# Layer normalisation on ScalarE's accumulator instead of VectorE's statistics, in a kernel with hand-written engine orders

## The chip, the cores and the metric
The kernel runs on one core of a Trainium2 chip. The metric is the device time of one execution in microseconds; three executions of the kernel before took 2475.67 to 2481.44 us, median 2475.96 us.

## The reference
A batch of 32 sequences with 256 tokens of 128 features passes through four blocks, each added to its input and each reading a layer-normalised copy of it:

```python
def _layernorm(x, axis=-1, eps=1e-05):
    m = jnp.mean(x, axis=axis, keepdims=True)
    v = jnp.var(x, axis=axis, keepdims=True)
    return (x - m) / jnp.sqrt(v + eps)

x = x + attention_0(_layernorm(x))   # 8 heads of one token mixed with each other, complex-valued encoding
x = x + ffn_0(_layernorm(x))         # silu(gate) * up, hidden size 384
x = x + attention_1(_layernorm(x))   # causal attention, 16 heads of 8, 256 tokens
x = x + ffn_1(_layernorm(x))         # 8 experts, each takes its 64 best tokens of a sequence
```

## The kernel before, in words
A sequence is held as two tiles of 128 tokens (partitions) by 128 features; T = 2 is the number of tiles. There are three parts: a setup of weights, a loop over the 32 sequences (here called batches), and an expert stage for the last block, which begins when all sequences have been through the loop.

The loop is a software pipeline of five stages: A (normalisation, projection to q, k, v, encoding and three layers of gates), C (the rest of the first attention, up to x1), B (first FFN, up to x2, and the normalisation of x2), E (scores, exponents and values of the second attention) and D (its output, x3, the normalisation of x3 and the routing logits). In one pass of the loop A works on batch b, C on b-1, B on b-2, E and D on b-3. Each stage is written as one Python generator for each engine; a `yield` ends a piece. Four strings set the order in which the pieces of the stages stand in the queue of an engine: `DVE_ORDER`, `ACT_ORDER`, `POOL_ORDER`, `PE_ORDER` ("C1A1C1" is one piece of C, one of A, one of C). Each engine runs its queue in that order, and waits on semaphores for the others. `together` unrolls the strings, `sequences` makes the loop with four passes ahead of it and three behind it. The numbers `DVE_A_STEPS` and so on count the increments of a semaphore that a stage uses on VectorE against itself.

A normalisation, before: VectorE runs `bn_stats` on each tile of the source, a small memset that keeps distance, and `bn_aggr` on each (mean and variance); GpSimd (`norm_scale`, L456) adds eps, negates the mean, raises to the power -0.5 and multiplies; ScalarE (`norm_apply`, L465) applies scale and bias. There are four a batch: A of the input (`x_land`), B1 of x1, B2 of x2, and D of x3.

Names used below: w0 to w7 are the eight products of the weighted sums (`weighted`, L627), six of them on VectorE and numbers 3 and 7 on GpSimd; TensorE sums each over the heads (L751), in the PSUM tile `pa`. L637 and L638 clip the result for each tile, L759 is the output projection, L612 writes x1. diag, add, ctrl and stadd are L522, L525, L527 and L529 of gate layers 1 and 2 on VectorE; cross and ctrl on GpSimd are L657 and L662, and they deliver what add and ctrl on VectorE need. state0 is L505, which waits for the power L649 on GpSimd. In E, `exp` is L923 and L924, a turn is L1036 on TensorE with the copy L931 on ScalarE, a maximum is L810 and L811 on VectorE. In D, L830 writes x3, L1086 transposes its normalised tile `xn_d`, L958 copies that, L1091 makes the logits. `pa` is shared by A, C and B, and semaphores take it from one to the next.

Of the kernel before, what the change touches and what calls it, by code (L numbers as in the profile page):

```python
# [27 lines left out]
EPS = 1e-5  # L28
SIGN = 0x80000000
# [19 lines left out]
POOL_ORDER = "A1C2B1A4C1B1A2C1D1C1D1"  # L49
ACT_ORDER = "E7A1E1A1E3A1E5B1E4B1E3C1A1E2B1E3C1E3B1A1E2C1E6A1E1B1D1C1D1C1D2"  # L50
PE_ORDER = "E4A1E1A1E6B1E4B1E7B1E2B1E3C1E1C1E1C1E1C1D1C1D1C1D1C2D2C2"
DVE_ORDER = "C1A1C1A1C1B1C1E1B1E1C2A1E1C1A1C1E1C2E1C2A1C1E1A1C1B1C1B1A1C1E1A1C2B1C1B1C1E1B1A1C1A1C2B2A2C2A1D2C2D3C1A2C2D2A1D2A1C1"


def build(nc, A, out):
# [8 lines left out]
    with ctx:  # L64
        def sb(name, shape, dt=F32):
            return ctx.enter_context(nc.sbuf_tensor(name, shape, dt))
# [80 lines left out]
        stats_a = first("stats_a", [P, T, 6])  # L147
        mv_a = first("mv_a", [P, T, 2])
# [33 lines left out]
        stats_b = first("stats_b", [P, T, 6])  # L182
        mv_b = first("mv_b", [P, T, 2])
# [9 lines left out]
        stats_d = first("stats_d", [P, T, 6])  # L193
        mv_d = first("mv_d", [P, T, 2])
# [280 lines left out]
        def vector_a(v, b):  # L475
            count_a[0] = 0
            L = lambda ins: link_a(v, b, ins)

            v.wait_ge(S("x_in"), 16 * b + 16)
            for t in range(T):  # L480
                count_a[0] += 1
                v.bn_stats(stats_a[:, t, :], x_land[:, t, :]).then_inc(S("dve_a"), 1)
            yield
            v.wait_ge(S("dve_a"), b * DVE_A_STEPS + 2)

            v.memset(spare[:, 3:4], 0.0).then_inc(S("dve_a"), 1)
            count_a[0] += 1
            for t in range(T):
                count_a[0] += 1
                v.bn_aggr(mv_a[:, t, :], stats_a[:, t, :]).then_inc(S("dve_a"), 1)  # L490
            yield
# [273 lines left out]
        def vector_norm(v, b, n, src):  # L765
            k0 = count_b[0]
            for t in range(T):
                count_b[0] += 1
                v.bn_stats(stats_b[:, t, :], src[:, t, :]).then_inc(S("dve_b"), 1)
            yield  # L770
            v.wait_ge(S("dve_b"), b * DVE_B_STEPS + k0 + 2)

            v.memset(spare[:, n:n + 1], 0.0).then_inc(S("dve_b"), 1)
            count_b[0] += 1
            for t in range(T):
                count_b[0] += 1
                v.bn_aggr(mv_b[:, t, :], stats_b[:, t, :]).then_inc(S("dve_b"), 1)
# [36 lines left out]
        def vector_d(v, b):  # L814
# [18 lines left out]
            v.wait_ge(S("x3_ready"), b + 1)  # L833
            for t in range(T):
                count_d[0] += 1
                v.bn_stats(stats_d[:, t, :], x3[:, t, :]).then_inc(S("dve_d"), 1)
            yield
            v.wait_ge(S("dve_d"), b * DVE_D_STEPS + 3)

            v.memset(spare[:, 2:3], 0.0).then_inc(S("dve_d"), 1)  # L840
            count_d[0] += 1
            for t in range(T):
                count_d[0] += 1
                v.bn_aggr(mv_d[:, t, :], stats_d[:, t, :]).then_inc(S("dve_d"), 1)
            yield

# [15 lines left out]
        def gpsimd_b(g, b):  # L862
            for n in range(2):
                g.wait_ge(S("dve_b"), b * DVE_B_STEPS + (5, 12)[n])
                norm_scale(g, 2 * b + n, mv_b, var_b, rstd_b, shift_b, "b_scale", "b_rstd")
                yield

        def gpsimd_d(g, b):
            g.wait_ge(S("dve_d"), b * DVE_D_STEPS + 6)
            norm_scale(g, b, mv_d, var_d, rstd_d, shift_d, "d_scale", "d_rstd")  # L870
# [573 lines left out]
```

## Time and profile before

| | |
|---|---|
| median of 3 runs | 2475.96 us |
| the profiled execution | 2466.69 us |
| its span, first to last instruction | 2464.9 us |
| busy TensorE / VectorE / ScalarE / GpSimd | 79% / 77% / 52% / 55% |
| mean granted TensorE clock | 0.902 |
| in the loop (1000 to 1500 us): VectorE, TensorE | 453.5 and 417.7 us of 500 |

The busy time is the sum of the durations of an engine's instructions; consecutive ones can overlap, so an engine may be free a little more than the difference suggests. The loop lasts until about 2080 us; the expert stage follows. Idle time in front of an instruction is put down to the instruction of another engine that released it last.

### The profile page before, as it was taken

How to read it: one execution, taken by the hardware profiler on the slowest of the kernel's cores; microseconds unless marked ns; L12 is line 12 of the kernel's file. 1: busy time of each engine (PE TensorE's matmuls, PEld its weight loads, DVE VectorE, ACT ScalarE, POOL GpSimd, SP SyncE). 2: the span in 40 equal slices, each digit the busy share in tenths (PEclk: the TensorE clock that was granted, in tenths of full speed). 3: DMA queues.
4: the chain of work that ended last, by engine and by line, in shares of the span. 5: the costliest groups of instructions: out<-in, count | busy, mean ns of one | idle time of the engine just before them, and what ended most of it. 6: DMA issues, size and time to landing. Idle time of an engine off the chain costs nothing.

```text
span 2464.9 us, 45044 instructions
## 1 busy us (share of the span) xinstructions
PE 1951.1 (79%) x15068; PEld 1517.4 (62%) x15068; DVE 1904.4 (77%) x3422; ACT 1272.1 (52%) x2989; POOL 1357.8 (55%) x1104
## 2 busy tenths in 40 slices
PE   1357888888888888888888888888888886199999
PEld 0346666666666666666666666666666663167777
DVE  4899999998999999899889999999988843402221
ACT  1126666655566655556555556665555554043332
POOL 2666666666666666666666666666666310544400
PEclk9679999988999988999988999998898896599999
DMA  3000000000000000000000000000000000112210
GB/s 93 3 7 9 10 11 9 9 9 9 9 9 9 9 9 9 9 9 9 9 9 9 9 9 9 9 9 9 9 9 6 7 6 9 45 33 69 61 42 26
DMA packets 64565, 39.38 MB, mean 16 GB/s; under 512 B 9350, under 2 KB 60431, under 8 KB 64528
## 3 DMA queue, kind: packets, MB, share of 16 engines
q1 hardware_dynamic: 54238, 26.30, 3.7%
q0 software_dynamic: 4096, 8.40, 1.3%
q10 hardware_dynamic: 6194, 4.21, 0.7%
q8 instruction: 21, 0.34, 0.1%
q14 instruction: 16, 0.13, 0.0%
HBM read 26.31 MB, written 12.58 MB: 16 GB/s over the span
## 4 chain that ended last, share of the span: by engine, by line
PE 27%; issue 22%; POOL 21%; DVE 20%; ACT 6%; ACTq 1%; DVEq 1%; POOLq 0%; DMA 0%
POOL arena L461 5%; PE pa L1296 5%; PE pd L1286 5%; POOL arena L657 5%; POOL arena L629 4%; DVE arena L811 4%; PE pb L1036 3%; POOL arena L458 2%; PE pa L732 2%; POOL arena L662 2%; POOL arena L463 1%; PE pa L759 1%; DVE arena L563 1%; POOL arena L1223 1%; DVE arena L558 1%
## 5 line engine op out<-in xcount | busy, mean ns | idle before, releaser
L751 PE MATMUL pa<-ident,arena 128*128 128x128 f32 x4096 | 528.9, 286 | 54.8 <-DVE arena L629 53.2
L751 PEld LDWEIGHTS pa<-ident,arena 128*128 128x128 f32 x4096 | 500.7, 200 | 72.6 <-DVE arena L629 36.5
L1036 PE MATMUL pb<-ident,arena 128*128 128x128 f32 x1536 | 292.7, 304 | 122.2 <-ACT arena L931 111.9
L1036 PEld LDWEIGHTS pb<-ident,arena 128*128 128x128 f32 x1536 | 188.4, 154 | 243.8 <-issue 158.5
L931 ACT ACTIVATE arena<-pb 128x384 f32<-128x384 f32 x512 | 252.3, 493 | 161.2 <-PE pb L1036 156.8
L657 POOL TENSOR_TENSOR arena<-state,c_cross 128x448 f32<-128x448 f32 x128 | 204.9, 1620 | 209.0 <-DVE state L518 204.7
L649 POOL TENSOR_TENSOR arena<-arena,neg_half 128x32 f32<-128x32 f32 x64 | 264.9, 4158 | 83.8 <-DVE arena L495 83.8
L629 POOL TENSOR_TENSOR arena<-arena 128x1024 f32<-128x1024 f32 x64 | 149.0, 2329 | 194.3 <-PE pa L751 194.3
L924 ACT ACTIVATE arena<-pd,arena 128x256 f32<-128x256 f32 x512 | 244.9, 478 | 0.0
L629 DVE TENSOR_TENSOR arena<-arena 128x1024 f32<-128x1024 f32 x192 | 236.5, 1257 | 2.9 <-PE pa L751 2.7
L458 POOL TENSOR_TENSOR arena<-arena,eps_t 128x2 f32<-128x2 f32 x128 | 106.0, 828 | 221.3 <-DVE arena L490 135.3
L923 ACT ACTIVATE arena<-pd,arena 128x128 f32<-128x128 f32 x512 | 188.5, 368 | 59.6 <-DVE arena L811 56.5
L1223 POOL DMA_INDIRECT arena<-xn_scratch,arena x128 | 122.0, 953 | 139.8 <-PE pa L1276 76.1
L1235 DVE TENSOR_TENSOR arena<-pa,arena 128x512 f32<-128x512 f32 x32 | 22.1, 692 | 221.5 <-PE pa L1296 221.5
L461 POOL TENSOR_TENSOR arena<-arena,neg_half 128x2 f32<-128x2 f32 x128 | 170.0, 1328 | 10.0
L811 DVE TENSOR_REDUCE arena<-pd 128x2 f32<-128x512 f32 x256 | 174.1, 680 | 0.0
L1027 PE MATMUL pd<-arena 32*128 32x256 f32 x1024 | 161.2, 392 | 0.0
L810 DVE TENSOR_REDUCE arena<-pd 128x2 f32<-128x256 f32 x256 | 106.3, 415 | 56.7 <-PE pd L1027 56.5
L559 DVE TENSOR_REDUCE arena<-arena 128x128 f32<-128x2048 f32 x64 | 146.0, 2281 | 0.1
L1266 ACT ACTIVATE arena<-pd,b 128x512 f32<-128x512 f32 x128 | 87.9, 687 | 108.9 <-PE pd L1286 108.4
L669 POOL TENSOR_TENSOR arena<-arena,state 128x1024 f32<-128x1024 f32 x64 | 131.4, 2075 | 0.7 <-DVE arena L553 0.7
L1024 PE MATMUL pd<-arena 32*128 32x128 f32 x1024 | 131.7, 335 | 0.0
(246 smaller groups left out, 4374.6 us busy)
## 6 DMA issues: line engine op xcount, KB each, us to landing
x_land<-in_L_attn_query SPq DMA_DIRECT2D x32, 128.0 KB, 2.1
arena<-in_L_attn_query SPq DMA_DIRECT2D x32, 128.0 KB, 2.1
x_scratch<-x SPq DMA_DIRECT2D x32, 128.0 KB, 1.8
xn_scratch<-xn_d SPq DMA_DIRECT2D x32, 128.0 KB, 1.8
arena<-x_scratch SPq DMA_DIRECT2D x16, 256.0 KB, 3.0
out_x<-arena SPq DMA_DIRECT2D x16, 256.0 KB, 2.4
w<-in_L_ffn_W ACTq DMA_DIRECT2D x1, 2048.0 KB
arena<-xn_scratch,arena POOLq DMA_INDIRECT x128, 2.5
```

The source lines that it names most:

```text
L458: g.tensor_tensor(var[:, :], mv[:, :, 1], eps_t[:, :], ALU.add).then_inc(S(steps), 1)
L461: g.tensor_tensor(rstd[:, :], var[:, :], neg_half[:, 0:2], ALU.pow).then_inc(S(steps), 1)
L629: return eng.tensor_tensor(wprod[:, k % NWP, :].rearrange("p (j i d) -> p j i d", j=NH, d=HD), amps[:, c, t, :, :].rearrange("p i j -> p j ...
L649: g.tensor_tensor(of_tile(rnorm)[:, :, c], of_tile(ssq)[:, :, c], of_tile(neg_half)[:, :, c], ALU.pow).then_inc(S("a_rnorm"), 1)
L657: ins = g.tensor_tensor(gate_r[:, c, :, :], st[:, 1 - c, :, HD:E], c_cross[:, l, 0:GW].unsqueeze(1).broadcast_to([P, 4, GW]), ALU.mult)
L751: mm = pe.matmul(pa[:, t, c * P:c * P + P], wprod[:, k % NWP, j * 128:j * 128 + 128], ident[:, :], start=(j == 0), stop=(j == NH - 1))
L811: v.tensor_reduce(n_max[:, 1, 2 * n:2 * n + 2], pd[:, s, 128:384], AX, ALU.min).then_inc(S("b_m"), 1)
L923: act.activation(p[:, 0:128], bank[:, 0:128], ACT.Exp, bias=n_max[:, 0, s:s + 1], scale=-1.0)
L924: act.activation(p[:, 128:384], bank[:, 128:384], ACT.Exp, bias=n_max[:, 1, s:s + 1], scale=-1.0)\
L931: act.activation(p_t[:, s % 8, :], pb[:, 0:384], ACT.Copy).then_inc(S("b_pt"), 1)
L1027: mm = pe.matmul(o[:, 128:384], q_m[rows_of, r, P:2 * P], k_t[rows_of, :], start=False, stop=True, skip_group_check=True)
L1036: mm = pe.transpose(pb[:, j * P:j * P + P], p_raw[:, s % 3, j * P:j * P + P], ident[:, :])
```

## The change
`bn_stats`, `bn_aggr` and the memset leave VectorE. ScalarE gets two passes over each tile instead: a Copy with the accumulator gives the sum, then a Square of x/sqrt(128) - mean/sqrt(128) with the accumulator gives the variance. Their elementwise outputs go to the tile that the normalised values overwrite later. GpSimd makes the mean between the two passes (`norm_mean`), and `norm_scale` loses the negation. Where a normalisation was one piece on GpSimd and one on ScalarE, it is now two and three. All four order strings are new.

```diff
-DVE_A_STEPS = 15
+DVE_A_STEPS = 10
 DVE_C_STEPS = 19
-DVE_B_STEPS = 12
-DVE_D_STEPS = 8
-POOL_ORDER = "A1C2B1A4C1B1A2C1D1C1D1"
-ACT_ORDER = "E7A1E1A1E3A1E5B1E4B1E3C1A1E2B1E3C1E3B1A1E2C1E6A1E1B1D1C1D1C1D2"
-PE_ORDER = "E4A1E1A1E6B1E4B1E7B1E2B1E3C1E1C1E1C1E1C1D1C1D1C1D1C2D2C2"
-DVE_ORDER = "C1A1C1A1C1B1C1E1B1E1C2A1E1C1A1C1E1C2E1C2A1C1E1A1C1B1C1B1A1C1E1A1C2B1C1B1C1E1B1A1C1A1C2B2A2C2A1D2C2D3C1A2C2D2A1D2A1C1"
+DVE_B_STEPS = 2
+DVE_D_STEPS = 3
+POOL_ORDER = "A1B1A1C1B1C1A4C1B1A1B1C1D1A1D1C1D1"
+ACT_ORDER = "E2B1A1E4A1E1B1E3A1E3A1B1E2A1E1B1E4C1E3A1E1B1E2C1E4A1B1E3C1E3B1E4B1C1A1D1B1D3C1D2"
+PE_ORDER = "E6A1E2A1E2B1E5B1E7B1E2B1E3C1E1C1E1C1E1C1D1C1D2C3D2C2"
+DVE_ORDER = "C4E1C1E1C2E1C1A2E1C4E1C2A1C1A1E1B1C1A1B1A1C2E1C1B2C1A1E1B1C3A1C1A1C1A1D2C1D1C2A3C2D2A1D1A1C1D1"
...
-        def norm_scale(g, u, mv, var, rstd, shift, steps, done):
-            g.tensor_tensor(var[:, :], mv[:, :, 1], eps_t[:, :], ALU.add).then_inc(S(steps), 1)
-            g.tensor_tensor(shift[:, :], mv[:, :, 0], minus_one[:, :], ALU.mult).then_inc(S(steps), 1)
+        def norm_sums(act, src, dst, total, done):
+            for t in range(T):
+                act.activation(dst[:, t, :], src[:, t, :], ACT.Copy, accum_out=total[:, t:t + 1]).then_inc(S(done), 1)
+        def norm_mean(g, total, shift, mean, steps, done):
+            g.tensor_tensor(shift[:, :], total[:, :], by_mean[:, :], ALU.mult).then_inc(S(steps), 1)
+            g.tensor_tensor(mean[:, :], total[:, :], by_scaled_mean[:, :], ALU.mult).then_inc(S(done), 1)
+        def norm_squares(act, src, dst, mean, var, done):
+            for t in range(T):
+                act.activation(dst[:, t, :], src[:, t, :], ACT.Square, bias=mean[:, t:t + 1], scale=ROOT_E,
+                               accum_out=var[:, t:t + 1]).then_inc(S(done), 1)
+        def norm_scale(g, u, var, rstd, shift, steps, done):
+            g.tensor_tensor(var[:, :], var[:, :], eps_t[:, :], ALU.add).then_inc(S(steps), 1)
             g.wait_ge(S(steps), 3 * u + 2)
             g.tensor_tensor(rstd[:, :], var[:, :], neg_half[:, 0:2], ALU.pow).then_inc(S(steps), 1)
             g.wait_ge(S(steps), 3 * u + 3)
             g.tensor_tensor(shift[:, :], shift[:, :], rstd[:, :], ALU.mult).then_inc(S(done), 1)
...
         def gpsimd_a(g, b):
-            g.wait_ge(S("dve_a"), b * DVE_A_STEPS + 5)
-            norm_scale(g, b, mv_a, var_a, rstd_a, shift_a, "a_scale", "a_rstd")
+            g.wait_ge(S("a_sums"), 2 * b + 2)
+            norm_mean(g, total_a, shift_a, mean_a, "a_scale", "a_mean")
+            yield
+            g.wait_ge(S("a_squares"), 2 * b + 2)
+            norm_scale(g, b, var_a, rstd_a, shift_a, "a_scale", "a_rstd")
             yield
...
         def scalar_a(act, b):
+            act.wait_ge(S("x_in"), 16 * b + 16)
+            norm_sums(act, x_land, xn_a, total_a, "a_sums")
+            yield
+            act.wait_ge(S("a_mean"), b + 1)
+            norm_squares(act, x_land, xn_a, mean_a, var_a, "a_squares")
+            yield
             act.wait_ge(S("a_rstd"), b + 1)
             norm_apply(act, x_land, rstd_a, shift_a, xn_a, "a_xn")
```

B1, B2 and D are changed in the same way. With the new strings the pieces stand as follows around the end of a pass. VectorE, new: w0 w1 w2 add1 w4 ctrl1 w5 stadd1, reciprocal, o_n, w6, x3, clip of tile 0 (two pieces), diag2 add2 ctrl2, clip of tile 1, logits maximum, stadd2, r_sum, v_enc, x1, r_inv. VectorE, before: w0 add1 w1 w2, statistics B2, ctrl1 stadd1 w4 w5 diag2, reciprocal, o_n, w6, L637, x3, statistics D, L638, add2 ctrl2, clip of tile 1, and on as above, with x1 last. GpSimd, new: mean A, mean B1, scale A, third product 0, scale B1, third product 1, two powers, cross1, ctrl1, w3, mean B2, cross2, scale B2, w7, mean D, ctrl2, scale D. GpSimd, before: scale A, two third products, scale B1, two powers, cross1, ctrl1, w3, scale B2, cross2, ctrl2, w7, scale D. ScalarE, new, at the start of a pass: copy of x2, copy of the transposed tile, sums B1, sums A, four copies of k and q, squares A, v, squares B1, exp0, exp1, turn 0, apply A; at its end: last turn, o_raw, squares B2, L719, gate square 2, o_t, apply B2, sums D, squares D, apply D.

## Rows read from the trace of the kernel before

**Rows 1.** The page's engine totals for the whole span.
```profile
PE 1951.1 (79%) x15068; PEld 1517.4 (62%) x15068; DVE 1904.4 (77%) x3422; ACT 1272.1 (52%) x2989; POOL 1357.8 (55%) x1104
```
**Rows 2.** The line that writes x1; busy time of one period (windows).
```profile
L612 DVE TENSOR_TENSOR arena<-arena,pa x32: 414/422/423, 125.6 to 1993.0; 128x256 f32<-128x256 f32 x32
...
1086.80:1147.40 60.60, 49.40 (x395) 38.52 (x396) 55.97 (x98) 36.05 (x89) 39.18 (x30) 0.95 0.03 9
```
**Rows 3.** Waits, 1026 to 1511 us: total, times, longest.
```profile
PE pd L1086 <- ACT xn_d L467: 11.5, 8, 1.6
...
DVE arena L612 <- PE pa L759: 9.3, 7, 1.6
```
**Rows 4.** Timeline of VectorE, 1058 to 1120 us: start, duration, instruction.
```profile
1060.02 1.21 DVE L629 TENSOR_TENSOR arena<-arena 128x1024 f32<-128x1024 f32 x1
...
1065.10 2.23 DVE L527 TENSOR_TENSOR arena<-arena 128x896 f32<-128x896 f32 x1
1067.37 1.10 DVE L529 TENSOR_TENSOR state<-state,arena 128x896 f32<-128x896 f32 x1
...
1076.37 0.42 DVE L830 TENSOR_TENSOR x<-arena,pd 128x256 f32<-128x256 f32 x1 [0.33 <-PE pd L1081]
1076.82 0.49 DVE L836 BATCH_NORM_STATS2 arena<-x 128x6 f32<-128x128 f32 x2
...
1077.51 0.66 DVE L638 SCALAR_TENSOR_TENSOR arena<-pa,arena 128x512 uint32<-128x512 uint32 x1
...
1086.34 0.42 DVE L612 TENSOR_TENSOR arena<-arena,pa 128x256 f32<-128x256 f32 x1 [1.35 <-PE pa L759]
...
1087.50 0.48 DVE L482 BATCH_NORM_STATS2 arena<-x_land 128x6 f32<-128x128 f32 x2
1087.90 0.41 DVE L555 TENSOR_TENSOR arena<-state 128x256 f32<-128x256 f32 x1
...
1097.76 0.95 DVE L494 TENSOR_REDUCE arena<-arena 128x48 f32<-128x768 f32 x1 [0.76 <-ACT arena L693]
...
1108.17 0.69 DVE L505 TENSOR_TENSOR state<-arena 128x512 f32<-128x512 f32 x1
```
**Rows 5.** Timeline of GpSimd, same stretch.
```profile
1066.34 1.04 POOL L458 TENSOR_TENSOR arena<-arena,eps_t 128x2 f32<-128x2 f32 x1
...
1069.62 4.05 POOL L657 TENSOR_TENSOR arena<-state,c_cross 128x448 f32<-128x448 f32 x2
1073.64 2.12 POOL L662 TENSOR_TENSOR arena<-arena 128x448 f32<-128x448 f32 x1
1075.71 2.20 POOL L629 TENSOR_TENSOR arena<-arena 128x1024 f32<-128x1024 f32 x1
1077.88 0.19 POOL L458 TENSOR_TENSOR arena<-arena,eps_t 128x2 f32<-128x2 f32 x1
...
1078.29 1.44 POOL L461 TENSOR_TENSOR arena<-arena,neg_half 128x2 f32<-128x2 f32 x1
1079.81 0.54 POOL L463 TENSOR_TENSOR arena<-arena 128x2 f32<-128x2 f32 x1
...
1100.96 8.28 POOL L649 TENSOR_TENSOR arena<-arena,neg_half 128x32 f32<-128x32 f32 x2 [2.71 <-DVE arena L495]
1115.62 2.35 POOL L657 TENSOR_TENSOR arena<-state,c_cross 128x448 f32<-128x448 f32 x2 [6.38 <-DVE state L518]
```
**Rows 6.** Timeline of ScalarE, same stretch.
```profile
1080.38 0.88 ACT L467 ACTIVATE xn_d<-x,arena 128x128 f32<-128x128 f32 x2 [5.57 <-POOL arena L463]
...
1090.37 0.47 ACT L911 ACTIVATE v_one<-pc 128x128 f32<-128x128 f32 x2
```
**Rows 7.** Timeline of TensorE, 1056 to 1092 us.
```profile
1068.31 2.05 PE L751 MATMUL pa<-ident,arena 128*128 128x128 f32 x16
...
1082.70 3.50 PE L759 MATMUL pa<-w_out_t,arena 128*128 128x128 f32 x16
```

More of the change, by code:

```diff
@@ L28 @@
 EPS = 1e-5
+ROOT_E = E ** -0.5
 SIGN = 0x80000000
@@ L146, in build @@
         x1 = first("x1", [P, T, E])
-        stats_a = first("stats_a", [P, T, 6])
-        mv_a = first("mv_a", [P, T, 2])
+        total_a = first("total_a", [P, T])
+        mean_a = first("mean_a", [P, T])
         var_a = first("var_a", [P, T])
@@ L179, in build @@
         clipped = first("clipped", [P, T, NC * P])
-        stats_b = first("stats_b", [P, T, 6])
-        mv_b = first("mv_b", [P, T, 2])
+        total_b = first("total_b", [P, T])
+        mean_b = first("mean_b", [P, T])
         var_b = first("var_b", [P, T])
@@ L192, in build @@
         xnt_e = first("xnt_e", [P, T * P])
-        stats_d = first("stats_d", [P, T, 6])
-        mv_d = first("mv_d", [P, T, 2])
+        total_d = first("total_d", [P, T])
+        mean_d = first("mean_d", [P, T])
         var_d = first("var_d", [P, T])
@@ L329, in setup_gpsimd @@
             step(g.memset(eps_t[:, :], EPS))
-            step(g.memset(minus_one[:, :], -1.0))
-            g.wait_ge(S("pool_setup"), 6)
+            step(g.memset(by_mean[:, :], -1.0 / E))
+            step(g.memset(by_scaled_mean[:, :], -ROOT_E / E))
+            g.wait_ge(S("pool_setup"), 7)
             for m in (ident, ident_b):
@@ L477, in vector_a @@
             L = lambda ins: link_a(v, b, ins)
[L479 to L491, printed above, removed]
             v.wait_ge(S("a_sq"), b + 1)
@@ L761, in tensor_c @@
             yield
[L765 to L777, printed above, removed]
         FFN_PARTS = ((slice(0, 2), slice(0, 2)), (slice(2, 3), slice(0, 1)))
@@ L832, in vector_d @@
             yield
[L833 to L845, printed above, removed]
             lg = pd[:, 3, 256:256 + T * NX].rearrange("p (t e) -> p t e", t=T)
@@ L863, in gpsimd_b @@
             for n in range(2):
[L864 to L865 removed]
+                g.wait_ge(S("b_sums"), 4 * b + 2 * n + 2)
+                norm_mean(g, total_b, shift_b, mean_b, "b_scale", "b_mean")
+                yield
+                g.wait_ge(S("b_squares"), 4 * b + 2 * n + 2)
+                norm_scale(g, 2 * b + n, var_b, rstd_b, shift_b, "b_scale", "b_rstd")
                 yield
         def gpsimd_d(g, b):
[L869 to L870 removed]
+            g.wait_ge(S("d_sums"), 2 * b + 2)
+            norm_mean(g, total_d, shift_d, mean_d, "d_scale", "d_mean")
+            yield
+            g.wait_ge(S("d_squares"), 2 * b + 2)
+            norm_scale(g, b, var_d, rstd_d, shift_d, "d_scale", "d_rstd")
             yield
@@ L877, in scalar_b @@
         def scalar_b(act, b):
+            act.wait_ge(S("x1_ready"), b + 1)
+            norm_sums(act, x1, xn_b, total_b, "b_sums")
+            yield
+            act.wait_ge(S("b_mean"), 2 * b + 1)
+            norm_squares(act, x1, xn_b, mean_b, var_b, "b_squares")
+            yield
             act.wait_ge(S("b_rstd"), 2 * b + 1)
@@ L887, in scalar_b @@
                 yield
-            act.wait_ge(S("b_rstd"), 2 * b + 2)
+            act.wait_ge(S("x2_ready"), b + 1)
             if not (isinstance(b, int) and b == 0):
                 act.wait_ge(S("e_xnt"), b)
+            norm_sums(act, x2, xn_e, total_b, "b_sums")
+            yield
+            act.wait_ge(S("b_mean"), 2 * b + 2)
+            norm_squares(act, x2, xn_e, mean_b, var_b, "b_squares")
+            yield
+            act.wait_ge(S("b_rstd"), 2 * b + 2)
             norm_apply(act, x2, rstd_b, shift_b, xn_e, "b_xn")
@@ L952, in scalar_d @@
             yield
+            act.wait_ge(S("x3_ready"), b + 1)
+            act.wait_ge(S("xn4_gone"), 16 * b + 1)
+            norm_sums(act, x3, xn_d, total_d, "d_sums")
+            yield
+            act.wait_ge(S("d_mean"), b + 1)
+            norm_squares(act, x3, xn_d, mean_d, var_d, "d_squares")
+            yield
             act.wait_ge(S("d_rstd"), b + 1)
-            act.wait_ge(S("xn4_gone"), 16 * b + 1)
             norm_apply(act, x3, rstd_d, shift_d, xn_d, "d_xn")
```

14 lines of the change are left out of this document (4 added, 10 removed).

## Prediction
> **What bounds the kernel now.** I read the page's engine totals first. VectorE is busy 77% of the whole span [rows 1], but that mixes stages. The attention/FFN loop is what the change touches, so I took its period next: the addition that writes x1 (one per batch) starts 32 times between 125.6 and 1993.0 us, which is 1867.4 / 31 = 60.2 us a batch, and 60.6 us in the two batches in the middle [rows 2]. One such period, 1086.8 to 1147.4, has VectorE busy 55.97 of 60.6 us, TensorE 49.4, GpSimd 39.2, ScalarE 36.0 [rows 2]. So VectorE is nearly the bound, but not quite: it stands idle some 5 to 6 us a batch (overlapping instructions are counted twice in its busy time), and the waits say where. The largest that matter are the end of the period: TensorE waits for the normalised tile xn_d 8 times in 8 batches, 11.5 us, and VectorE waits for the output projection before x1, 9.3 us [rows 3]. So the period ends in a chain: x3, its normalisation, the transposition of xn_d, the logits, the two output projections, x1. TensorE's queue has the projections behind the logits, therefore the latency of normalisation D is in the period.
>
> I count from two marks: w0, the first weighted product (1060.02), and the end of x1 (1086.34 + 0.42 = 1086.76). w0 to x1 is 26.7 us (the tail); x1 to the next w0 is 60.6 - 26.7 = 33.9 us (the front) [rows 4].
>
> **What is removed.** Four normalisations a batch (A, two B, D), each two statistics, a memset, two aggregates on VectorE. What they occupy is read from start to start: all of D's 1076.82 to 1077.51, 0.69, which holds the small gaps of its own dependency; A's statistics alone 1087.50 to 1087.90, 0.40 [rows 4]. Between these I take 0.62, near the whole one, and 0.56 for A and B1 whose two pieces have other work between: 2.4 to 2.5 us a batch. If all came through: 2.5 x 32 = 80 us.
>
> **What is added on ScalarE.** Sixteen activations of 128x128 a batch. None like them is in the trace with an accumulator. Near rows: two plain copies of this size take 0.47 us together, two applications with scale and bias from memory 0.88 [rows 6]. Bounds for a pair: 0.47 from below; 1.4 from above (the 0.88 and again half of it for reading out). I take 0.88 for both kinds. That is 8 x 0.88 = 7.0 us more on an engine that has 24 us idle, so total load is no bound; order is. Copy and Square already run in this kernel between Exp and Sqrt, so no table load is added.
>
> The Trainium skill ("ScalarE: Activation LUTs", What ACT_TABLE_LOAD costs) gives 186 ns + 0.833 ns an element and 93 ns for each pointer operand, so by estimate 0.39 us for one Square and 0.69 for an overlapped pair, without a price for the accumulator; with it the squares would cost 0.2 less a pair and the sum 0.2 to 0.4 us less a batch.
>
> **What is added on GpSimd.** Before, four operations of a normalisation in one piece; now five in two pieces, with a round trip to ScalarE between. A small operation costs 0.19 us when it starts at 1077.88 and 1.04 at 1066.34 [rows 5]. At 1066.34 VectorE was in a product with both inputs in SBUF (L527, 2.23 us from 1065.10); at 1077.88 it ran L638, which reads PSUM [rows 4]. So the two operations of a mean cost between 0.38 and 1.23; I take 0.6, nearer the lower row, since in the new order VectorE is often waiting there.
>
> **The front.** Old: statistics A start 0.7 us after x1 (1087.50) and the squares-sum reduction of A (L494) starts at 1097.76, 11.0 after x1, having waited 0.76 [rows 4]. New: ScalarE first has the copy of xnt, sums B1 and sums A (to 1.9 after x1), GpSimd both means (to 3.4), then k, q copies, squares A (to 4.5), v, squares B1, and exp0 comes at 5.6, near where it was. Scale A is over at 7.5, A applied at 8.3. But the A transposition is now behind two turns, apply B1 waits for GpSimd (scale A, third product, scale B1) until 12.3 and stands in front of the copy of qkv. So L494 can start at 14.9, 3.9 later. VectorE gets there at 14.2: the new order puts a product, a maximum and a reduction, 4.4 us, in front, less 1.1 removed. Then GpSimd's first power takes 5.4 of the 8.28 us [rows 5] beside 5.6 us of VectorE work, and state0 starts at 21.7 against 1108.17 - 1086.76 = 21.4. Between state0 and w0 nothing is removed. Adding the pieces one by one gives w0 at 33.3 to 34.3; I take 33.8 (old 33.9). So the 1.1 us removed here is spent on waits.
>
> **The tail, from w0.** Order on VectorE now: w0 w1 w2 add1 w4 ctrl1 w5 stadd1, reciprocal, o_n, w6, x3. TensorE needs 1.95 to 2.05 for each summed product [rows 7]: first 1.3 to 3.4, second to 5.4, and w4 must wait for the second (a wait of 1.0). w4 ends 6.6, ctrl1 7.6, w5 8.8, stadd1 9.8; the old stadd1 ended at 8.4 (1068.4) [rows 4]. x3 comes early, at 14.3 instead of 16.8, since it now stands before the clip. But its normalisation waits for GpSimd, whose order is mean B2, cross2, scale B2, w7, mean D, ctrl2, scale D. Old: cross2 from 9.6, ctrl2, w7, scale D at 17.9, applied 21.2 [rows 5, 6]. New:
> - cross2 starts with stadd1 at 9.85; the pair takes 2.35 (1115.62) to 4.05 (1069.62) [rows 5]; VectorE has one two-input product in it, so 3.2: 13.1.
> - scale B2, three operations, 0.19 + 1.44 + 0.2 and gaps, 2.0: 15.1. Before it was done when cross2 started at 1069.62; this is the new stretch. ScalarE applies B2 to 16.0 and sums D to 16.9.
> - w7, 2.2: 17.3. Mean D, 0.6: 17.9.
> - ScalarE's squares D, 0.9, are beside ctrl2 on GpSimd (2.12 at 1073.64, I take 1.9): 19.8. Scale D 2.1: 21.9. Apply 0.9: 22.8.
> - From the end of apply to x1 as before: 1081.26 to 1086.76, 5.5 (transposition, copy, logits, projections of 3.5 [rows 7]): 28.3.
> VectorE's work after x3 (clips, diag2, add2, ctrl2, stadd2) is 8 to 9 us in a window of 14, so it hides nothing more and sets nothing. Tail 28.3 against 26.7: +1.6. Bounds: all GpSimd rows at their low end give 26.1 (-0.6), all at the high end 31.5 (+4.8).
>
> **Sum.** -0.1 + 1.6 = +1.5 us a batch; 31 periods and the last batch's own tail: 32 x 1.5 = +48 us. The profiled execution took 2466.7 (span 2464.9 plus 1.8 around it), so 2515 for it; it is 9.3 below the median of the runs, 2475.96, so 2524 there. Start and expert stage are unchanged.
>
> **Rivals.**
> - The relief comes through (faster). Place: GpSimd between stadd1 and scale D. If small operations start at 0.19 and cross2 takes 2.35, the tail is 26.1 and the front 33.3: 59.4, -1.2 x 32 = -38, 2438; if the order also fills the waits, at most -80, 2396. For it: VectorE is the busiest engine and has more idle time between, so fewer collisions. Against: the chain then needs the low row at five places. It decides from a GpSimd chain of 12.1 - 1.6 = 10.5 us between stadd1 and the end of scale D (old 11.9 from 68.4 to 80.35).
> - The two cancel: a tail of 26.7 to 27.0, 2476. It needs half of those low rows.
> - Everything collides: tail 31.5, accumulator pairs of 1.4 delay exp0 by 1 us, so +5 x 32 = +160, 2636. For it: 1.04, 0.54 and 4.05 all occur on GpSimd now [rows 5]. Against: they coincide with VectorE's dense stretches, and the new order has gaps there.
> The Trainium skill ("SBUF — State Buffer", Who interferes with whom) says that a VectorE instruction with two SBUF inputs contends with a GpSimd instruction that reads SBUF, and that whoever issues first keeps the shared ports. The trace agrees with its 1.04 against 0.19. Taken for every small operation it gives this last case.
>
> **How the numbers follow.** Forecast (+0.4 to +3 a batch, 2490 to 2572) 0.48; relief 0.32; cancelled 0.12; all collides 0.08. About 0.3% (7.4 us) is what a measurement of this kernel can tell from no change. So faster 0.32, same 0.12, slower 0.56. Range 2415 to 2590: it leaves out the far ends of the relief and of the collisions. The likeliest case's own range is 2490 to 2572.
>
> **What would show it.** In the changed profile: the period between x1 additions 62.1 (60.6 before); x3 some 2.5 us earlier after w0, but xn_d 1.6 later; scale B2 behind cross2 on GpSimd; L494 waiting for ScalarE near 0.7 us; VectorE's idle time a batch up from some 6 to 10. The step fails if the time from stadd1 to the end of scale D is under 10.5 us, or if w0 comes under 33 us after x1; a pair of accumulating activations outside 0.47 to 1.4 breaks the price on ScalarE.

## The result, and the profile after

The changed kernel takes 2586.46 us (median of 4 runs, 2585.76 to 2587.28) against 2478.7 us before on the same chip (2475.67 to 2484.97): ratio 1.0431, 95% interval 1.0408 to 1.0455. It is 107.8 us slower. The forecast was slower by 48 us; the direction was right, the size was under half of it, and the time lies just inside the range of 2415 to 2590.

The profiled execution took 2586.29 us, with a span of 2584.5 and a mean granted clock of 0.871 (before: 2466.69, 2464.9, 0.902).

First the page's engine totals, then the line that writes x1, then one period of the loop (columns: window, length, busy time and instructions of TensorE, its weight loads, VectorE, ScalarE, GpSimd; granted clock, DMA share, GB/s). They answer to [rows 1, 2]:

```profile
PE 2014.9 (78%) x15068; PEld 1557.5 (60%) x15068; DVE 1833.0 (71%) x2782; ACT 1456.5 (56%) x4013; POOL 1358.4 (53%) x1233
...
L614 DVE TENSOR_TENSOR arena<-arena,pa x32: 418/421/422, 128.7 to 2103.6; 128x256 f32<-128x256 f32 x32
...
1085.50:1150.00 64.50, 52.45 (x394) 40.60 (x394) 52.85 (x77) 41.69 (x121) 39.89 (x34) 0.90 0.03 8
```

The x1 writes span 2103.6 - 128.7 = 1974.9 us, 63.71 a batch, against 60.24 before. 3.47 us x 31 = 107.6 us. The spans of the two profiled executions differ by 119.6 us; the other 12 lie ahead of the first x1 (3) and behind the last (9). So the loss is in the loop. VectorE gave up work as the change says (1904 to 1833 us in the whole span), and it waits more than it gave up.

Waits of 1000 to 1510 us (who waits for whom: total us, times, longest), answering to [rows 3]:

```profile
PE pd L1086 <- ACT xn_d L483: 31.9, 8, 4.1
...
DVE arena L614 <- PE pa L770: 14.6, 8, 1.9
```

TensorE's wait for the normalised x3 went from 11.5 to 31.9 us in eight batches, 2.6 us a batch. This is the wait that closes the period. Why it grew is read from GpSimd's timeline (start, duration, instruction, idle time before):

```profile
1131.09 3.22 POOL L662 TENSOR_TENSOR arena<-state,c_cross 128x448 f32<-128x448 f32 x2 [2.16 <-DVE state L531]
1134.26 0.19 POOL L475 TENSOR_TENSOR arena<-arena,eps_t 128x2 f32<-128x2 f32 x1
...
1135.62 2.02 POOL L631 TENSOR_TENSOR arena<-arena 128x1024 f32<-128x1024 f32 x1
1137.59 1.04 POOL L465 TENSOR_TENSOR arena<-arena,by_mean 128x2 f32<-128x2 f32 x1
1138.74 2.04 POOL L667 TENSOR_TENSOR arena<-arena 128x448 f32<-128x448 f32 x1
1140.75 0.19 POOL L475 TENSOR_TENSOR arena<-arena,eps_t 128x2 f32<-128x2 f32 x1
...
1142.73 0.20 POOL L479 TENSOR_TENSOR arena<-arena 128x2 f32<-128x2 f32 x1
```

Between stadd1 and the end of scale D (1131.01 to 1142.93) GpSimd has cross2, scale B2 (1134.26 to 1135.66), w7, mean D, ctrl2 and scale D in one queue without a gap. x3 is ready at 1135.01, 14.6 us after w0 and 7.9 us before scale D ends. VectorE, from one w0 to the next:

```profile
1120.42 3.48 DVE L631 TENSOR_TENSOR arena<-arena 128x1024 f32<-128x1024 f32 x3
...
1125.89 1.98 DVE L631 TENSOR_TENSOR arena<-arena 128x1024 f32<-128x1024 f32 x1 [0.98 <-PE pa L762]
...
1134.59 0.42 DVE L821 TENSOR_TENSOR x<-arena,pd 128x256 f32<-128x256 f32 x1 [1.28 <-PE pd L1081]
...
1149.57 0.42 DVE L614 TENSOR_TENSOR arena<-arena,pa 128x256 f32<-128x256 f32 x1 [1.90 <-PE pa L770]
...
1165.82 0.95 DVE L496 TENSOR_REDUCE arena<-arena 128x48 f32<-128x768 f32 x1 [1.01 <-ACT arena L704]
...
1172.78 0.69 DVE L507 TENSOR_TENSOR state<-arena 128x512 f32<-128x512 f32 x1
...
1185.09 3.48 DVE L631 TENSOR_TENSOR arena<-arena 128x1024 f32<-128x1024 f32 x3
```

w0 1120.42, end of x1 1149.99, next w0 1185.09: a tail of 29.6 (26.7 before) and a front of 35.1 us (33.9 before) in this pass. Windows of TensorE alone (window, length, busy time and instructions, granted clock, DMA share, GB/s) show what follows the wait:

```profile
1140.00:1143.80 3.80, 0.00 (x0) 1.00 0.00 0
1143.80:1150.00 6.20, 5.49 (x24) 0.58 0.07 21
...
1156.00:1165.00 9.00, 7.30 (x27) 0.64 0.05 15
```

TensorE stands still here for all of 3.8 us and then gets a granted clock of 0.58, a mean over two levels: 0.50 (1.2 GHz) from 1146 to 1150, and 1.00 (2.4 GHz) at first. The output projections (16 matmuls) take 3.76 us instead of 3.50 in the pass that the prediction took, the logits 1.02 instead of 0.61. In the front the turns run at 0.64. Over 1000 to 1500 us the clock is 0.89, before it was 0.92.

One pass isn't the mean of all. Averages of the timelines over the passes from 300 to 1900 us, cut into the front (end of x1 to w0), the time from w0 until D is applied (ScalarE has written xn_d), and the time from there to the end of x1:

| | front | w0 to D applied | from there to x1 | projections |
|---|---|---|---|---|
| before | 34.07 | 21.52 | 4.96 | 2.91 |
| after | 34.72 | 23.48 | 5.98 | 3.65 |

The three parts grew by 0.65, 1.96 and 1.02 us. In the kernel before, the projections take 2.03 us in 9 of 26 passes and 2.5 to 4.5 in the others; in the kernel after, 3.4 to 3.8 in all.

### The profile page after: what moved, and what is told of

Same layout as the page of the kernel before. It is cut to its first block, busy times and chain, and to the rows that moved or that the text cites. A ratio compares the mean times of both kernels' runs of the same rounds, so it can differ in the third digit from the quotient of the medians.

```text
span 2584.5 us, 45501 instructions
## 1 busy us (share of the span) xinstructions
PE 2014.9 (78%) x15068; PEld 1557.5 (60%) x15068; DVE 1833.0 (71%) x2782; ACT 1456.5 (56%) x4013; POOL 1358.4 (53%) x1233
## 4 chain that ended last, share of the span: by engine, by line
PE 34%; POOL 20%; DVE 17%; issue 16%; ACT 11%; ACTq 1%; DVEq 1%; POOLq 0%; DMA 0%
POOL arena L631 5%; PE pa L1296 4%; PE pd L1286 4%; PE pa L770 4%; POOL arena L662 4%; PE pb L1036 4%; DVE arena L802 3%; POOL arena L477 3%; PE pa L743 3%; DVE arena L565 3%; POOL arena L465 2%; PE pb L1004 2%; ACT arena L902 2%; PE pd L1027 2%; PE pd L1024 1%
## 5 line engine op out<-in xcount | busy, mean ns | idle before, releaser
L762 PE MATMUL pa<-ident,arena 128*128 128x128 f32 x4096 | 510.2, 282 | 54.0 <-DVE arena L631 48.4
L762 PEld LDWEIGHTS pa<-ident,arena 128*128 128x128 f32 x4096 | 487.7, 197 | 68.8 <-issue 36.6
L1036 PE MATMUL pb<-ident,arena 128*128 128x128 f32 x1536 | 299.9, 310 | 150.4 <-ACT arena L925 113.0
L631 DVE TENSOR_TENSOR arena<-arena 128x1024 f32<-128x1024 f32 x192 | 251.7, 1336 | 49.5 <-PE pa L762 48.8
L662 POOL TENSOR_TENSOR arena<-state,c_cross 128x448 f32<-128x448 f32 x128 | 172.3, 1366 | 198.9 <-DVE state L520 109.5
L917 ACT ACTIVATE arena<-pd,arena 128x128 f32<-128x128 f32 x512 | 192.5, 376 | 23.7 <-DVE arena L802 21.7
L465 POOL TENSOR_TENSOR arena<-arena,by_mean 128x2 f32<-128x2 f32 x128 | 105.7, 826 | 147.3 <-ACT arena L461 97.0
L1027 PE MATMUL pd<-arena 32*128 32x256 f32 x1024 | 171.5, 414 | 0.0
L477 POOL TENSOR_TENSOR arena<-arena,neg_half 128x2 f32<-128x2 f32 x128 | 147.7, 1154 | 10.0
L1024 PE MATMUL pd<-arena 32*128 32x128 f32 x1024 | 139.1, 351 | 0.0
```

Source lines behind the costliest of these rows:

```text
L631: return eng.tensor_tensor(wprod[:, k % NWP, :].rearrange("p (j i d) -> p j i d", j=NH, d=HD), amps[:, c, t, :, :].rearrange("p i j -> p j ...
L662: ins = g.tensor_tensor(gate_r[:, c, :, :], st[:, 1 - c, :, HD:E], c_cross[:, l, 0:GW].unsqueeze(1).broadcast_to([P, 4, GW]), ALU.mult)
L762: mm = pe.matmul(pa[:, t, c * P:c * P + P], wprod[:, k % NWP, j * 128:j * 128 + 128], ident[:, :], start=(j == 0), stop=(j == NH - 1))
L917: act.activation(p[:, 0:128], bank[:, 0:128], ACT.Exp, bias=n_max[:, 0, s:s + 1], scale=-1.0)
L1024: pe.matmul(o[:, 0:128], q_m[rows_of, r, 0:P], k_t[rows_of, 0:P], start=False, stop=True, skip_group_check=True)
L1027: mm = pe.matmul(o[:, 128:384], q_m[rows_of, r, P:2 * P], k_t[rows_of, :], start=False, stop=True, skip_group_check=True)
```

## Experiments

Theories at the start. **One:** the new order of GpSimd's queue puts scale B2 and D's mean, with its round trip to ScalarE, into the chain that closes the period; the loss is latency in a queue. **Two** (a rival inside it): the orders are at fault and the normalisation on ScalarE is nearly free. **Three:** the lower clock is the cause, not a consequence. **Four:** the time goes into the accumulating activations, or into contention of small operations. The recorded expectations number them otherwise: their theory 3, the added work alone, is four here, and the clock has no number there.

Each run is given as its ratio to the kernel before on the same chip and as the period between x1 writes (before 60.24, after 63.71). The ratio is the measure of the whole: on some chips the kernel before took about 2570 instead of 2475 us. The traces of variants from those chips have the extra outside the loop: from the last x1 to the end it is 576 us in e1, 472 in the trace of the kernel before. A sum of periods is the measure of a part.

### The old normalisation in the new orders (e1), and the new one in the old orders (e7, e8)

```diff
 # e1, on the kernel before; the three other strings take the places of the change too
-POOL_ORDER = "A1C2B1A4C1B1A2C1D1C1D1"
+POOL_ORDER = "A1C1B1C1A4C1A1B1C1A1D1C1D1"
```

> The old normalisation (statistics on VectorE) with the four new orders; the statistics stand again near their old places, the pieces for sums, squares and means are left out. Theory 1 (the loss is the chain on GpSimd and ScalarE from the last gate addition to the normalised x3, with scale B2 now in front of product 7, the mean of D and the round trip added): scale B2 stays in the chain, the mean of D and some of the front go, so about 62 us a batch, 2510 to 2530 us. Theory 2 (the new orders alone cost it: products 4 and 5 and the gate steps placed so that VectorE waits): 2560 to 2590. Theory 3 (only the work added on ScalarE and GpSimd costs, the orders are fine): 2470 to 2485.

Measured: 2667.9 against 2576.7 us, ratio 1.0353 (1.0310 to 1.0395), period 63.41. With `bn_stats` and `bn_aggr` back on VectorE and only the orders new, 3.17 of the 3.47 us are there, more than the 62 us a batch that theory one had forecast for this run. The orders carry most of the loss, and theory four falls as its main cause.

```diff
 # e7, on the kernel after: old places of the pieces as near as they go, in all four strings
-POOL_ORDER = "A1B1A1C1B1C1A4C1B1A1B1C1D1A1D1C1D1"
+POOL_ORDER = "A2C1B1C1B1A4C1B1A2C1D2B1C1D1"
```

> The new normalisation in the orders of the kernel before; sums A stand first in a pass on ScalarE (before x1 is there), scale B2 behind scale D. Theory 2 (the orders carry the loss): near the kernel before or below it, -60 to +10 us. Theory 3 (the work on ScalarE and the round trips carry it, whatever the order): +40 us or more.

Measured: ratio 1.0532 (1.0460 to 1.0604), period 64.20. If the orders carry the loss, this was to be near the kernel before; by its own expectation the result speaks for theory four. But the place of the loss is another one. On average the front is 37.1 us (34.7 after) and the tail 27.8 (29.5 after). GpSimd's third product (stage C) now starts as the pass begins, and runs beside VectorE's first work of the same stage. VectorE and GpSimd:

```profile
1085.63 2.29 DVE L557 TENSOR_TENSOR arena<-state 128x256 f32<-128x256 f32 x1
```

```profile
1085.60 2.04 POOL L674 TENSOR_TENSOR arena<-arena,state 128x1024 f32<-128x1024 f32 x1
```

VectorE's operation of 0.43 us in the kernel after takes 2.29 us, all through GpSimd's 2.04 us. It happens in every second pass, so it is 0.9 us on average of the 2.4 by which the front is longer than in the kernel after; the rest stays open. The test changes two things at once, and so doesn't give the price of the normalisation; e9 below bounds it for A and both B. e8, the same with the output projections ahead of the logits in TensorE's order, behaved alike:

> e7_new_norm_old_order with the projections first as in e5. If D's chain is the last thing at the end of a period once VectorE has 2.5 us less to do, this is the fastest of all: 2 to 3 us a batch under the kernel before, -60 to -100 us. If TensorE's own queue or E's chain sets it, no better than e6 and e7.

Measured: 1.0515 (1.0444 to 1.0587), period 63.96.

### The place of scale B2 (e2, e11, e12)

```diff
 # e2, on the kernel after; on ScalarE the application of B2 goes behind the copy of the normalised D
-POOL_ORDER = "A1B1A1C1B1C1A4C1B1A1B1C1D1A1D1C1D1"
+POOL_ORDER = "A1B1A1C1B1C1A4C1B1A1C1D1A1D1B1C1D1"
```

> The changed kernel with one piece of GpSimd (scale B2) moved behind scale D, and the application of B2 on ScalarE moved behind the copy of the transposed x3. Theory 1: scale B2 (1.4 us) leaves the chain to x1, and TensorE's wait for xn_d shrinks, 1.5 to 2 us a batch, 2520 to 2540 us. Theory 2 and 3: nothing that they blame is touched, 2580 to 2590.

Measured: 2599.18 against 2576.7 us, ratio 1.0091 (1.0056 to 1.0126), period 61.07. Three small GpSimd operations behind scale D instead of before w7, with the application of B2 on ScalarE that follows them, give back 2.64 of the 3.47 us. GpSimd's timeline of e2:

```profile
1090.87 3.22 POOL L662 TENSOR_TENSOR arena<-state,c_cross 128x448 f32<-128x448 f32 x2 [2.16 <-DVE state L531]
1094.05 2.01 POOL L631 TENSOR_TENSOR arena<-arena 128x1024 f32<-128x1024 f32 x1
1096.02 0.38 POOL L465 TENSOR_TENSOR arena<-arena,by_mean 128x2 f32<-128x2 f32 x1
```

w7 follows cross2 at once, and the first operation of mean D takes 0.38 instead of 1.04 us.

```diff
 # e11, on e1
-POOL_ORDER = "A1C1B1C1A4C1A1B1C1A1D1C1D1"
+POOL_ORDER = "A1C1B1C1A4C1B1A1C1A1D1C1D1"
```

> e1_old_norm_new_order (statistics on VectorE, new orders) with scale B2 ahead of cross2 on GpSimd, as in the kernel before. The chain theory: cross2, scale B2, product 7 lose one link, about 2 us of the 3.17 a batch: 61.3, +30 to +40 us against the kernel before. If the new orders cost elsewhere: 63, +80 us or more.

Measured: 1.0118 (1.0085 to 1.0151), period 61.07, which is 2.34 less than e1. With the old normalisation scale B2 can go ahead of cross2, as it stood before. So its place matters with the new normalisation and with the old. The reverse, in the kernel before:

```diff
 # e12, on the kernel before
-POOL_ORDER = "A1C2B1A4C1B1A2C1D1C1D1"
+POOL_ORDER = "A1C2B1A4C1A1B1A1C1D1C1D1"
```

> The kernel before with one change: scale B2 behind cross2 on GpSimd instead of ahead of it. Nothing is added to any engine. The chain theory: cross2 starts some 1.1 us earlier but product 7 and scale D come 1 to 2.3 us later: +1 to +2.3 us a batch, +30 to +75 us. If VectorE's load sets the period of the kernel before: 0 to +10 us.

Measured: 2541.41 to 2562.06 against 2473.32 us, ratio 1.0310 (1.0257 to 1.0364), period 63.32: one piece of one string moved, no added work, and 3.08 of the 3.47 us. GpSimd and TensorE's wait:

```profile
1051.53 4.13 POOL L657 TENSOR_TENSOR arena<-state,c_cross 128x448 f32<-128x448 f32 x2 [2.16 <-DVE state L529]
1055.62 1.04 POOL L458 TENSOR_TENSOR arena<-arena,eps_t 128x2 f32<-128x2 f32 x1
...
PE pd L1086 <- ACT xn_d L467: 21.4, 8, 2.7
```

In these orders the place of scale B2 is necessary for most of the loss (e2, e11) and sufficient for most of it (e12). The 2.3 us that e12's expectation allowed for the chain were about right: D is applied 2.25 us later. The rest, 0.74 us, is the stretch from there to x1, with projections of 3.50 instead of 2.91 us on average.

### D's round trip to ScalarE (e4, e9)

```diff
 # e4, on the kernel after: D alone has its statistics on VectorE again
...
-            g.wait_ge(S("d_sums"), 2 * b + 2)
-            norm_mean(g, total_d, shift_d, mean_d, "d_scale", "d_mean")
-            yield
...
+            g.wait_ge(S("dve_d"), b * DVE_D_STEPS + 6)
...
```

> The changed kernel with normalisation D back on VectorE's statistics (0.69 us of VectorE after x3, the mean on GpSimd and two passes on ScalarE removed); A, B1 and B2 stay on ScalarE. Theory 1: the mean of D (1.2 us) leaves the GpSimd chain, about 1.3 to 1.8 us a batch, 2525 to 2545 us. Theory 3: a quarter of the added work goes, 2560. Theory 2: 2586.

Measured: 1.0309 (1.0274 to 1.0345), period 62.77, 0.94 less than after, and less than the 1.3 to 1.8 that was expected.

e9 is e4 with scale B2 late, as in e2:

> The changed kernel with both repairs of e2 and e4: normalisation D on VectorE's statistics, scale B2 behind scale D on GpSimd and apply B2 behind the copy of the transposed x3. If the two costs (2.64 us a batch from e2, 0.94 from e4) are separate links of one chain they add: 63.71 - 3.58 = 60.1 us between x1 additions, within 10 us of the kernel before. If either repair already brings out the next limit (VectorE, E's chain, the front), 60.8 to 61.1, +18 to +27 us.

Measured: 2476.02 against 2473.32 us, ratio 0.9999 (0.9976 to 1.0022), period 60.19. The two parts add up: 2.64 + 0.94 = 3.58 was to be had, 63.71 - 60.19 = 3.52 came. A and both B on ScalarE, D on VectorE, is as fast as the kernel before and not faster.

### The projections ahead of the logits (e5, e6)

```diff
 # e6, on the kernel before; ScalarE's and VectorE's ends of the strings follow
-PE_ORDER = "E4A1E1A1E6B1E4B1E7B1E2B1E3C1E1C1E1C1E1C1D1C1D1C1D1C2D2C2"
+PE_ORDER = "E4A1E1A1E6B1E4B1E7B1E2B1E3C1E1C1E1C1E1C1D1C1D1C1D1C4D2"
```

> The kernel before (statistics on VectorE, its own orders) with the same move of the projections. Same question for the kernel before: if D's chain sets the end there too, x1 comes 1 to 2.7 us earlier, 30 to 80 us faster in all. If VectorE's load (54.6 of 60.6 us) sets the period, 0 to 10 us.

> The changed kernel with scale B2 and apply B2 behind D's, and with the two output projections ahead of D's transposition and logits on TensorE; the copy of the second sums (Abs) ahead of apply D on ScalarE; the logits' maximum and what follows behind x1 on VectorE. If normalisation D is what sets the end of a period, x1 no longer waits for it: 1 to 2 us a batch better than e2_scale_b2_late (61.07 between x1 additions), so 59 to 60 and 10 to 40 us faster than the kernel before. If the place of scale B2 alone was the fault and VectorE or the front sets the rest (theory 2), no gain over e2: 20 us slower than before.

Measured: e6 1.0129 (1.0061 to 1.0198), period 61.25; e5 (scale B2 late as well) 1.0354 (1.0283 to 1.0425), period 62.72, worse than e2's 61.07. Both were to gain, and both lost. x1 no longer waits for the normalisation, but D's transposition and logits now stand between x1 and the next scores, and VectorE waits there: for L1027 14.0 us in e6 where it waited 3.4 before. In e6 the tail is 2.4 us shorter and the front 3.4 longer: the latency moved from the end of the pass to its beginning.

### The clock (e3, e13, e15, e16)

```diff
 # e3 (FILL = 12), e13 (36) on the kernel after; e15 (18) on e9; e16 (10) on the kernel before
+            for _ in range(FILL):
+                pe.transpose(pd[:, 0, 384:512], ident[:, :], ident[:, :])
```

The transpositions go into a free part of `pd` while TensorE would wait for xn_d; nobody reads them.

> The changed kernel with 12 transpositions of the identity into unused PSUM columns on TensorE ahead of its wait for xn_d (3.3 us of a wait of 4.1). It adds work and removes nothing. If the lower granted clock after that wait (0.58 from 1143.8 to 1150, against 0.75 in the same stretch before) is part of the loss: 0.5 to 1 us a batch faster, 2555 to 2570 us. If the clock costs nothing: 2586 or a little more.

Measured: 1.0422 (1.0384 to 1.0460), period 63.72. Twelve take 1.47 us and not the 3.3 that were planned, so 2.85 us of the wait were left, and the clock behind it was 0.50 again. It tells nothing of theory three.

> The changed kernel with 36 filler transpositions into unused PSUM columns ahead of TensorE's wait for xn_d (0.11 us each, 3.96 us of a wait of 4.15). If the idle time in front lowers the clock for logits, projections and the next q and k: tail 0.7 us and front 0.4 us a batch shorter, period 62.6 to 62.9 (63.71). If the clock falls regardless, or the projections are not on the path: 63.7.

Measured: 1.0294 (1.0254 to 1.0334), period 62.38. TensorE's timeline of e13, and the windows of 1000 to 1500 us of e13 and of after:

```profile
1056.41 4.09 PE L1086 MATMUL pd<-ident 128*128 128x128 f32 x36
...
1061.66 2.03 PE L771 MATMUL pa<-w_out_t,arena 128*128 128x128 f32 x16
...
1000.00:1500.00 500.00, 432.17 (x3433) 341.04 (x3432) 435.49 (x607) 333.48 (x959) 300.24 (x272) 0.92 0.03 8
```

```profile
1000.00:1500.00 500.00, 406.39 (x3034) 314.48 (x3035) 411.46 (x592) 323.46 (x938) 306.47 (x268) 0.89 0.03 8
```

The filled wait is followed by projections of 2.03 us at the full clock instead of 3.76, and the mean clock rises from 0.89 to 0.92. So 1.33 us a batch of the period can be had back through the clock. On average the time from D's application to x1 falls from 5.98 to 4.27 us, while D is applied at the same place (23.55 after w0, 23.48 without) and the front stays (34.73, 34.72): in the front TensorE is at 0.50 in e13 too, from 1074 to 1077. So the filler acts on this one stretch.

It doesn't stand beside the queue's 3.5: e9, with no filler, gives all of 3.5 back. The unfilled wait is followed by the lower clock, and theory three holds as an amplifier of the queue. It is a large part, though: in e2, D is applied 1.12 us earlier than in the kernel after, and the stretch behind is 1.70 shorter (4.28).

> e9_d_vector_b2_late with 18 fillers (2.0 us of its wait of 2.2). If the clock follows the filling: 59.6 to 59.9. If not: 60.2.

Measured: 1.0094 (1.0063 to 1.0125), period 61.10, against 60.19 without the filler. The forecast failed because the wait that was to be filled is gone. TensorE and ScalarE of e15:

```profile
1094.41 5.52 PE L766 MATMUL pa<-ident,arena 128*128 128x128 f32 x48
1099.77 2.13 PE L1099 MATMUL pd<-ident 128*128 128x128 f32 x18
1101.73 0.38 PE L1102 MATMUL pd<-ident,xn_d 128*128 128x128 f32 x2
```

```profile
1098.98 0.88 ACT L487 ACTIVATE xn_d<-x,arena 128x128 f32<-128x128 f32 x2 [5.18 <-POOL arena L873]
```

xn_d is ready at 1099.86, when TensorE comes out of the weighted sums; the 18 transpositions then hold it for 1.9 us more. In all 25 passes they end at 22.9 us after w0, and D is applied at 20.9. e9 has passes of two kinds: in 19 of 26 TensorE is through with the sums at 19.3 and D is applied at 21.5, in 7 both come at 20.9; in e15 all are of the second kind, and why is open. The projections at full clock (2.03 us, 2.45 in e9) give back only a part. In the kernel before, ten of them do help:

> The kernel before with 10 fillers (1.1 us of its wait of 1.3 to 1.6). Same: 59.9 to 60.1 if the clock follows, 60.24 if not.

Measured: 2545.85 against 2570.61 us, ratio 0.9916 (0.9890 to 0.9943), period 59.66, clock 0.95 instead of 0.92 in the loop. What decides is whether the wait is there: in e16 the ten transpositions end at 21.4 us after w0 and D is applied at 21.6, and all projections take 2.03 us.

### What VectorE does meanwhile (e10, e14, e17)

```diff
 # e14, on e9: ctrl1 and stadd1 stand ahead of w4
-DVE_ORDER = "...C1B2C1A1E1B1C3A1C1A1C1A1D2C1D3C2A3C2D2A1D1A1C1D1"
+DVE_ORDER = "...C1B2C1A1E1B1C3A3C2D2C1D3C2A3C2D2A1D1A1C1D1"
```

> e9_d_vector_b2_late with ctrl1 and stadd1 of gate layer 1 ahead of product 4 on VectorE, which there waits 1.0 to 2.6 us for TensorE. cross2 on GpSimd can start 2 to 3 us earlier. If that start is a link of the chain to x1: period 58.5 to 59.6 (60.19), faster than both kernels by 20 to 50 us. If product 7 and its sum on TensorE set the tail in e9: 60.2.

Measured: 2550.48 against 2570.61 us, ratio 0.9932 (0.9905 to 0.9958), period 59.48, 0.71 less than e9. cross2 starts 1.9 us earlier, D is applied 0.5 us earlier, and the kernel is faster than both.

> e14_e9_stadd1_early with 10 fillers ahead of the wait for xn_d. If clock and chain are separate: 59.48 - 0.58 = 58.9 us a batch, ratio to the kernel before 0.982 to 0.988. If the filler only moves the stretch at the lower clock to another place, as in e15: 59.5 to 60.5, ratio 0.993 to 1.005.

Measured: 0.9969 (0.9948 to 0.9990), period 60.02. e14 and the filler of e16 don't add up. In the passes where D is applied at 20.4 us after w0, the ten transpositions hold TensorE until 22.0, as in e15.

e10 is e11 with the reduction of A's squares ahead of two pieces of VectorE's queue:

> e11_old_norm_b2_ahead with the sum of squares of q, k, v (L494) and its maximum moved ahead of the second large reduction on VectorE. If its place is what makes the front 1.2 us longer: a gain of 0.5 to 0.8 us a batch over e11 (it is ready 0.7 us before VectorE takes it). If the pieces of A on TensorE hold it: 0 to 0.2.

Measured: 1.0290 (1.0256 to 1.0325), period 62.37 against 61.07. It was to gain and lost 1.3 us. VectorE's waits of 1000 to 1500 us in e10:

```profile
DVE arena L494 <- ACT arena L693: 12.4, 8, 1.7
```

The expectation took the input as ready 0.7 us early; it isn't. VectorE now stands still for 1.55 us a pass until ScalarE has squared q, k and v, with the large reduction behind it in the queue; e11 has this wait not at all. The front is 36.7 us instead of 35.0.

## Why the prediction was right in direction and short in size

Point by point, for the pass with w0 at 1120.42 (absolute times; this pass is 64.7 us long, the mean 63.7):

| step of the prediction | forecast | measured |
|---|---|---|
| x3 after w0 | 14.3 | 14.6 |
| stadd1 ends after w0 | 9.8 | 10.6 |
| cross2 | 3.2 | 3.22 |
| scale B2 | 2.0 | 1.4 |
| mean D | 0.6 | 1.2 |
| stadd1 to the end of scale D | 12.1, decides from 10.5 | 11.9 |
| D applied after w0 | 22.8 | 23.4 |
| from there to x1 | 5.5 | 6.15 |
| tail | 28.3 | 29.6 |
| L496 starts after x1 | 14.9 | 15.8 |
| state0 starts after x1 | 21.7 | 22.8 |
| front | 33.8 | 35.1 |

**Right:** the chain. The forecast placed scale B2 behind cross2, called it the new stretch, and made the chain's length the deciding point; e2, e11 and e12 show that this placement alone is worth 2.3 to 3.1 us a batch. The round trip of D, worth 0.94 (e4), was in the sum too. From the end of stadd1 to the end of scale D it took 11.9 us, as in the kernel before; what moved is its start, 10.6 after w0 instead of 8.4, and the forecast had that too (9.8). The two rivals on the fast side needed a chain under 10.5 us, and it took 11.9.

**Right:** the price on ScalarE. The tile's rows (median ns between lowest and highest):

```profile
L461 ACT ACTIVATE xn_d<-x x64: 292/293/309, 238.9 to 2197.9; 128x128 f32<-128x128 f32 x64
L461 ACT ACTIVATION_READ_ACCUMULATOR xn_d<-x x64: 185/187/189, 239.1 to 2198.1; 128x1 f32 x64
L470 ACT ACTIVATE xn_d<-x,arena x64: 384/394/403, 240.6 to 2199.2; 128x128 f32<-128x128 f32 x64
```

A pair with its read-outs takes 0.68 (sums) and 0.87 us (squares), within 0.47 to 1.4; the squares at the 0.88 taken, the sums 0.2 below it. ScalarE went from 1272 to 1456 us.

**Wrong: the step "From the end of apply to x1 as before, 5.5", a change of nothing.** It took TensorE's transposition, logits and projections over at the durations of one pass of the trace before. On average this stretch grew from 4.96 to 5.98 us, +1.02, and it is the largest of the missed terms. The prediction itself had TensorE waiting longer for xn_d, and didn't ask what TensorE would run at afterwards. e13 shows that the stretch hangs on this wait: with the wait filled it is 4.27 us. e13's 1.33 us a batch is no measure of the miss, since it also takes away what the kernel before pays: there the same move gives 0.58 (e16).

**Wrong: the front at -0.1.** It grew by 0.65 us on average. L496 came 0.9 and state0 1.1 us later in the pass of the table than forecast. It isn't the normalisation: with the old one in the new orders the front is 35.15 (e1) and 35.04 (e11). It isn't the clock behind the wait for xn_d either (e13). Which piece of the new orders does it stays open; the turns did run at 0.64 here, against 0.81 in the like window before, and no run isolates that. A small slip besides: the 14.2 us at which VectorE was to reach L494 are about 11.0 + 4.4 - 1.1, with the old wait of 0.76 left in; it got there at 14.8.

**Too small: the time until D is applied, +1.6 forecast, +1.96 measured.** In 18 of 24 passes the weighted product w4 took 1.98 and not some 1.2 us. Its wait for TensorE was 0.98 us, as forecast. Its row (1125.89 to 1127.87) stands above; GpSimd's:

```profile
1123.82 2.97 POOL L631 TENSOR_TENSOR arena<-arena 128x1024 f32<-128x1024 f32 x1 [6.13 <-PE pa L762]
1126.75 1.17 POOL L465 TENSOR_TENSOR arena<-arena,by_mean 128x2 f32<-128x2 f32 x1
1127.88 1.04 POOL L466 TENSOR_TENSOR arena<-arena,by_scaled_mean 128x2 f32<-128x2 f32 x1
```

When w4 started, GpSimd's product w3 still ran, to 1126.79, and w4 ended 1.08 us after that. The mean's first operation started then, and ended just behind w4. So the rows fit w4 held by w3, and the mean held by w4: a cost of the new order. They fit less with w4 held by the mean, which started 0.86 us into w4's 1.98. No run isolates it. The forecast had priced contention for GpSimd's side alone. The Trainium skill ("SBUF — State Buffer", Who interferes with whom) says that a VectorE instruction with two SBUF inputs contends with a GpSimd instruction that reads SBUF; w4's 1.98 us and e7's 2.29 us agree. In most of the other passes w4 takes 1.23 us, but only after a wait of 2.62 for TensorE.

The three terms, 1.02 + 0.75 + 0.36, make the 2.1 us that are missing to the 3.63 us of these passes (1.5 forecast). The direction was no luck: the queue that it named is where most of the loss is. But between a quarter (0.74 of 2.99 us in e12) and over half (1.70 of 2.82 in e2) of what its placement costs lies in the stretch behind D's application, where the sum had nothing.

**Where the relief went.** VectorE had 71 us less busy time in the whole span, 2.2 us a batch against 2.4 to 2.5 forecast, and all of it became waiting. In the new orders the new normalisation of A and B is worth about 0.88 us (e11 61.07 against e9 60.19, which also differ in the place of scale B2), and the rest of the new orders costs 0.83 (e11 against before). The parts along this path are: scale B2 +2.64, D's round trip +0.94, other order changes +0.83, A and B on ScalarE -0.88, which makes +3.53 against 3.47. Of this sum only the first two are a test, since e9 measured them together (3.52).

Open: which piece makes the front longer, and when TensorE's clock falls; the runs show it behind waits of 1.3 us (before) to 4.1 us (after), and in 9 of 26 passes of the kernel before not at all.

## What to carry to other kernels

Taking work off the busiest engine gained nothing here, since the period is closed by a chain of another one; look first at which queue holds the last wait, and what stands in it between the input and the output of that wait. When a forecast makes TensorE wait longer, don't carry its durations behind the wait over from the old trace: give a second term for the clock, and take the old durations from several passes. When work is split into pieces with a round trip, the place of every small piece in each in-order queue is part of the price: here three operations of 1.4 us together cost 2.6 us a batch. Before filling a wait, look at all passes: where the wait is missing, the filler is the delay.

## What the runs showed of the hardware that was not expected

- An activation with an accumulator is two instructions, 293 or 394 ns and 187 ns for reading out.
- Work that nobody needs can make a kernel faster: ten transpositions, 1.25 us a batch, raised the granted clock from 0.92 to 0.95 and took 0.8% off the kernel before (e16). Eighteen of them in e9, where in each pass they ran past the moment at which xn_d was ready, made it 0.9% slower (e15).
- A VectorE operation of 0.43 us took 2.29 us while a GpSimd product of 2.04 us ran (e7).
